# Cross-attention on Trainium2: probabilities transposed on TensorE, or in 32x32 blocks on VectorE and carried through DRAM

## What is computed

```python
q = _split_heads(hidden_states @ Wq.T, H)                  # (2, 20, 2048, 32)
k = _split_heads(text @ Wk.T, H); v = _split_heads(text @ Wv.T, H)
out_text = _merge_heads(_attend(q, k, v, sm_scale))        # softmax(q k^T / sqrt(32)) v
k_ip = _split_heads(ip @ Wk_ip.T, H); v_ip = _split_heads(ip @ Wv_ip.T, H)
out_ip = _merge_heads(_attend(q, k_ip, v_ip, sm_scale))
out = (out_text + IP_SCALE * out_ip) @ Wo.T + bo + residual
```

## Time and profile before

| | |
|---|---|
| median of 3 runs | 603.59 us |
| the profiled execution's own time | 606.17 us |
| its span in the trace | 604.1 us |
| PE busy | 583.6 us (97%) |
| DVE busy | 445.9 us (74%) |
| ACT busy | 312.6 us (52%) |
| POOL busy | 311.0 us (51%) |
| DMA, mean over the span | 76 GB/s |

### The profile page before, as it was taken

One profiled execution on the slowest core, in us unless ns is written; L12 is line 12 of the kernel. 1 busy time (PEld: TensorE's weight loads), 2 busy tenths in 40 slices (PEclk: granted clock), 3 DMA queues, 4 the chain that ended last, 5 costly groups with the idle time before them and its releaser, 6 DMA issues.

```text
span 604.1 us, 14571 instructions
## 1 busy us (share of the span) xinstructions
PE 583.6 (97%) x5634; PEld 516.3 (85%) x5634; DVE 445.9 (74%) x576; ACT 312.6 (52%) x594; POOL 311.0 (51%) x341
## 2 busy tenths in 40 slices
PE   8997878999999999999999999999999999999988
PEld 7997757888888888888888888888888888888867
DVE  0028576888788888878888887888888888788872
ACT  0223644565646555565655565555555565645541
POOL 0033436455574656475555647564746555574460
PEclk9998898999999999999999999999999999999999
DMA  8992001112121212112121212121211212111101
GB/s 296 414 374 79 1 1 28 63 36 88 44 81 44 87 35 82 39 46 76 43 87 35 86 39 84 35 87 43 68 53 35 87 35 87 44 37 44 36 18 62
DMA packets 29401, 46.20 MB, mean 76 GB/s; under 512 B 3392, under 2 KB 24512, under 8 KB 29120
## 3 DMA queue, kind: packets, MB, share of 16 engines
q1 hardware_dynamic: 29376, 45.84, 22.3%
HBM read 35.34 MB, written 10.49 MB: 76 GB/s over the span
## 4 chain that ended last, share of the span: by engine, by line
PE 92%; DVE 3%; ACT 2%; DMA 1%; issue 1%; SPq 0%; POOL 0%; ACTq 0%
PE q_ps L580 23%; PE x_ps L580 22%; PE main_ps L616 11%; PE s_ps L604 9%; PE pv_ps L635 8%; PE pv_ps L633 7%; PE s_ps L725 3%; PE pv_ps L624 3%; PE pv_ps L725 2%; PE main_ps L725 1%; DMA stage<-wk_in 1%; DVE row_sum L503 1%; ACT probs L363 1%; PE s_ps L672 1%; ACT p_main L368 1%
## 5 line engine op out<-in xcount | busy, mean ns | idle before, releaser
L305 POOL TENSOR_TENSOR probs<-probs,row_inv 128x616 f32<-128x616 f32 (+1 forms) x160 | 159.7, 1020 | 228.9 <-DVE row_inv L506 228.9
L503 DVE TENSOR_REDUCE row_sum<-probs 128x16 f32<-128x1232 f32 x80 | 114.9, 1436 | 45.7 <-ACT probs L363 45.7
L363 ACT ACTIVATE probs<-probs 128x616 f32<-128x616 f32 x160 | 113.8, 719 | 60.4 <-DVE probs L495 60.4
L368 ACT ACTIVATE p_main<-main_ps 122x512 f32<-122x512 f32 x160 | 94.3, 589 | 88.4 <-PE main_ps L616 88.1
L487 DVE TENSOR_REDUCE row_max<-s_ps 128x16 f32<-128x1232 f32 x80 | 115.3, 1441 | 31.7 <-PE s_ps L604 31.7
L495 DVE TENSOR_TENSOR probs<-s_ps,row_max 128x616 f32<-128x616 f32 x160 | 120.5, 795 | 2.7
L616 PE MATMUL main_ps<-ident,probs 128*122 128x128 f32 x640 | 96.1, 273 | 4.5 <-ACT p_main L368 4.5
L580 PE MATMUL q_ps<-x_hi,wq_hi 128*128 128x256 f32 x400 | 88.9, 320 | 0.0
L387 ACT ACTIVATE attn_hi<-pv_ps 128x256 fp32r<-128x256 f32 x80 | 30.9, 387 | 91.4 <-PE pv_ps L635 91.0
L616 PEld LDWEIGHTS main_ps<-ident,probs 128*122 128x122 f32 x640 | 73.1, 138 | 6.0 <-ACT p_main L368 5.9
L580 PE MATMUL x_ps<-attn_hi,wo_hi 128*128 128x256 f32 x375 | 75.5, 299 | 0.8 <-ACT y L382 0.8
(11 more groups left out here) (71 smaller groups left out, 774.0 us busy)
## 6 DMA issues: line engine op xcount, KB each, us to landing
x_raw<-x_in SPq DMA_DIRECT2D x16, 640.0 KB, 3.8
res<-x_in SPq DMA_DIRECT2D x75, 128.0 KB, 2.0
y_out<-res SPq DMA_DIRECT2D x75, 128.0 KB, 1.7
stage<-wk_in SPq DMA_DIRECT2D x6, 640.0 KB, 8.2
stage<-wv_in SPq DMA_DIRECT2D x6, 640.0 KB, 9.7
wq_raw<-wq_in SPq DMA_DIRECT2D x1, 1600.0 KB, 10.1
wo_raw<-wo_in SPq DMA_DIRECT2D x1, 1600.0 KB, 7.3
stage<-wk_in SPq DMA_DIRECT2D x4, 320.0 KB, 5.8
```

Of the source, the lines that this page charges most:

```text
L305: nc.gpsimd.tensor_tensor(rows[:, :, keys], rows[:, :, keys], row_inv[:, u.slot, :, br].unsqueeze(2) .broadcast_to([P, GROUP * SUB, size]) ...
L363: nc.scalar.activation(probs[:, u.slot, heads], probs[:, u.slot, heads], ACT.Exp).then_inc(exp_done, 1)
L368: nc.scalar.activation(p_main[0:MAIN, :, s * P:(s + 1) * P], main_ps[0:MAIN].rearrange("p (j n) -> p j n", j=GROUP), ACT.Copy).then_inc(ma ...
L503: nc.vector.tensor_reduce(row_sum[:], by_row(probs[:, u.slot].rearrange("p j s n -> p j (s n)")), AXIS.X, ALU.add).then_inc(sum_done, 1)
```

## The change

All 154 keys now take one other way. `normalise` writes all of the second branch. DVE then turns the probabilities of a unit in 32x32 blocks (`turn`, three instructions, into `turned`): each block of 32 query rows and 32 keys is transposed in place of its four partition groups. One DMA (`bounce`) writes the 640 KB of `turned` to the DRAM tensor `bounce_d`, and eight DMAs (`load_turned`) read it back: four of 128 KB into `p_main`, which put the 32 keys of each of four blocks on their own 32 partitions, and four of 32 KB into `p_rest`, for the last 26 keys of each head, padded to 32. All nine are issued by SP. The transposes of PE, their identity operand and `keep_main` of ACT, `keep_rest` of DVE and `normalise_rest` of POOL are gone. `weigh_values` reads `p_main` and `p_rest` with strides, and now works on unit `u-3`; the output chunk is that of `u-8`.

The softmax is split by heads: for the first two heads ACT reads `s_ps` itself, in eight instructions of 77 keys, with the negated row maximum as bias and the row sum as accumulator output (`exp_direct`). The other two heads go as before, through one `take_max` and one `exp`; DVE sums only these. `find_max` is two instructions of two heads each.

```diff
-REST = D
-MAIN = BLK - REST
+BLOCKS = P // D
+MAIN = BLOCKS * D
+REST = BLK - MAIN
+ROW = GROUP * SUB * D
 VALUES = 2 * BATCHES
 PASSES = 3
 STEPS_OF_PRODUCT = PASSES * GROUPS
-OUT_LAG = 6
+OUT_LAG = 8
+VALUE_LAG = 3
 Q_AHEAD = 2
 PAIR = 2
-HALF = D // 2
+PARTS = 3
...
+        probs_flat = sbuf("probs", [P, 2, GROUP * SUB * BLK + MAIN])
+        probs = probs_flat[:, :, 0:GROUP * SUB * BLK].rearrange("p i (j s n) -> p i j s n", j=GROUP, s=SUB)
+        turned = sbuf("turned", [P, 2, BLOCKS + 1, GROUP * SUB, D])
+        p_main = sbuf("p_main", [P, GROUPS, BLOCKS, GROUP, SUB, D])
+        p_rest = sbuf("p_rest", [P, GROUPS, BLOCKS, SUB, D])
+        bounce_d = nc.dram_tensor("bounce_d", (GROUPS, P, BLOCKS + 1, ROW), F32, kind="Internal").ap()
...
+            def bounce(u):
+                wait(sp, p_turned, u.number(PARTS, PARTS))
+                sp.dma_start(bounce_d[u.g].rearrange("p b n -> p (b n)"),
+                             turned[:, u.slot].rearrange("p b q k -> p (b q k)")).then_inc(bounced, DMA)
+            def load_turned(u):
+                wait(sp, bounced, u.number(DMA, DMA))
+                for b in range(BLOCKS):
+                    sp.dma_start(p_main[rows_of(b), u.g].rearrange("k a j s n -> k a (j s n)"),
+                                 bounce_d[u.g, :, b].rearrange("(a k) n -> k a n", a=BLOCKS)
+                                 ).then_inc(p_loaded[u.g], DMA)
+                for j in range(GROUP):
+                    cols = slice(j * SUB * D, (j + 1) * SUB * D)
+                    sp.dma_start(p_rest[rows_of(j), u.g].rearrange("k a s n -> k a (s n)"),
+                                 bounce_d[u.g, :, BLOCKS, cols].rearrange("(a k) n -> k a n", a=BLOCKS)
+                                 ).then_inc(p_loaded[u.g], DMA)
             def emit(u):
                 ahead, old, new = u.tile_plus(2), u.plus(-OUT_LAG - 2), u.plus(GROUPS - OUT_LAG - 3)
+                if u.plus(-2).exists():
+                    load_turned(u.plus(-2))
                 if new.exists() and not (new.fixed and new.number() >= LAST.number()):
                     load_residual(new)
                 if old.exists():
                     store(old)
+                if u.plus(-1).exists():
+                    bounce(u.plus(-1))
                 if u.g == 2 and ahead.exists():
                     wait(sp, x_lo_done, u.tile(1, 2))
                     sp.dma_start(x_raw[:], x_d[ahead.t, ahead.batch]).then_inc(x_loaded, DMA)
...
+            final = LAST.plus(GROUPS - 1)
+            load_residual(LAST.plus(-1))
+            store(LAST.plus(-5))
+            load_turned(final.plus(-1))
+            store(LAST.plus(-4))
+            bounce(final)
+            store(LAST.plus(-3))
+            load_turned(final)
+            store(LAST.plus(-2))
...
-                for br, keys in enumerate((slice(0, KEYS), slice(KEYS, MAIN))):
+                for br, keys in enumerate((slice(0, KEYS), slice(KEYS, BLK))):
...
-            def exp(u, half):
-                heads = slice(half * PAIR, (half + 1) * PAIR)
-                wait(act, s_drained, u.number(2, half + 1))
-                nc.scalar.activation(probs[:, u.slot, heads], probs[:, u.slot, heads], ACT.Exp).then_inc(exp_done, 1)
-            def keep_main(u, s):
-                wait(act, main_turned, u.number(SUB, s + 1))
-                nc.scalar.activation(p_main[0:MAIN, :, s * P:(s + 1) * P],
-                                     main_ps[0:MAIN].rearrange("p (j n) -> p j n", j=GROUP), ACT.Copy
-                                     ).then_inc(main_kept, 1)
+            def exp_direct(u):
+                wait(act, max_done, u.number(2, 1))
+                for j in range(PAIR):
+                    rows = probs[:, u.slot, j].rearrange("p s n -> p (s n)")
+                    for i in range(SUB * BRANCHES):
+                        cols = slice(i * KEYS, (i + 1) * KEYS)
+                        done = nc.scalar.activation(rows[:, cols], s_ps[:, j, cols], ACT.Exp,
+                                                    bias=row_neg[:, j, i:i + 1], accum_out=row_sum[:, j, i:i + 1])
+                done.then_inc(direct_done, 1)
+            def exp(u):
+                wait(act, sub_done, u.number(1, 1))
+                rows = probs[:, u.slot, heads_of(1)]
+                nc.scalar.activation(rows, rows, ACT.Exp).then_inc(exp_done, 1)
...
-                ahead, nxt, last = u.tile_plus(2), u.plus(Q_AHEAD), u.plus(-1)
+                ahead, nxt = u.tile_plus(2), u.plus(Q_AHEAD)
                 chunk = u.plus(-OUT_LAG)
-                if u.plus(-2).exists():
-                    attn_high(u.plus(-2))
-                exp(u, 0)
-                if chunk.exists():
-                    exp(u, 1)
-                    keep_main(last, 0)
-                else:
-                    keep_main(last, 0)
-                    exp(u, 1)
+                exp_direct(u)
+                exp(u)
+                if u.plus(-VALUE_LAG).exists():
+                    attn_high(u.plus(-VALUE_LAG))
                 if nxt.exists():
                     keep_q(nxt)
-                keep_main(last, 1)
                 if chunk.exists():
                     add_bias(chunk)
...
-            def find_max(u):
-                wait(dve, s_ready, u.number(1, 1))
-                nc.vector.tensor_reduce(row_max[:], by_row(s_ps[:, :, 0:SUB * BLK]), AXIS.X, ALU.max
-                                        ).then_inc(max_done, 1)
-            def take_max(u, half):
+            def find_max(u, half):
                 if half == 0:
-                    wait(dve, max_done, u.number(1, 1))
-                heads = slice(half * PAIR, (half + 1) * PAIR)
+                    wait(dve, s_ready, u.number(1, 1))
+                nc.vector.tensor_reduce(row_neg[:, heads_of(half)], by_row(s_ps[:, heads_of(half), 0:SUB * BLK]),
+                                        AXIS.X, ALU.max, negate=True).then_inc(max_done, 1)
+            def take_max(u):
+                wait(dve, max_done, u.number(2, 2))
+                heads = heads_of(1)
                 nc.vector.tensor_tensor(by_row(probs[:, u.slot, heads].rearrange("p j s n -> p j (s n)")),
                                         by_row(s_ps[:, heads, 0:SUB * BLK]),
-                                        row_max[:, heads].unsqueeze(3).broadcast_to([P, PAIR, SUB * BRANCHES, KEYS]),
-                                        ALU.subtract).then_inc(s_drained, 1)
+                                        row_neg[:, heads].unsqueeze(3).broadcast_to([P, PAIR, SUB * BRANCHES, KEYS]),
+                                        ALU.add).then_inc(sub_done, 1)
+            def turn(u, part):
+                wait(dve, p_done, u.number(BRANCHES, min(part + 1, BRANCHES)))
+                if part == 0:
+                    wait(dve, bounced, u.number(DMA, -DMA))
+                first, end = (0, 2, BLOCKS, BLOCKS + 1)[part:part + 2]
+                rows = probs_flat[:, u.slot, first * D:first * D + GROUP * SUB * BLK].rearrange("p (q n) -> p q n", n=BLK)
+                nc.vector.transpose(turned[:, u.slot, first:end],
+                                    rows[:, :, 0:(end - first) * D].rearrange("p q (b k) -> p b q k", k=D)
+                                    ).then_inc(p_turned, 1)
             def invert(u):
-                wait(dve, exp_done, u.number(2, 2))
-                nc.vector.tensor_reduce(row_sum[:], by_row(probs[:, u.slot].rearrange("p j s n -> p j (s n)")),
+                wait(dve, exp_done, u.number(1, 1))
+                nc.vector.tensor_reduce(row_sum[:, heads_of(1)],
+                                        by_row(probs[:, u.slot, heads_of(1)].rearrange("p j s n -> p j (s n)")),
                                         AXIS.X, ALU.add).then_inc(sum_done, 1)
                 wait(dve, sum_done, u.number(1, 1))
+                wait(dve, direct_done, u.number(1, 1))
                 nc.vector.reciprocal(row_inv[:, u.slot].rearrange("p (j s) r -> p j (s r)", j=GROUP), row_sum[:]).then_inc(inv_done, 1)
...
             def emit(u):
-                find_max(u)
                 for half in range(2):
-                    take_max(u, half)
-                if u.plus(-2).exists():
-                    attn_low(u.plus(-2))
+                    find_max(u, half)
+                take_max(u)
+                if u.plus(-1).exists():
+                    for part in range(PARTS):
+                        turn(u.plus(-1), part)
                 invert(u)
-                keep_rest(u.plus(-1))
+                if u.plus(-VALUE_LAG).exists():
+                    attn_low(u.plus(-VALUE_LAG))
...
                 wait(pe, q_done, u.number(1, 1))
-                wait(pe, s_drained, u.number(2))
+                wait(pe, direct_done, u.number())
...
+            def weigh_values(u):
+                wait(pe, p_loaded[u.g], u.tile((BLOCKS + GROUP) * DMA, (BLOCKS + GROUP) * DMA))
+                wait(pe, attn_lo_done, u.number())
```

(31 more changed lines are left out.)

135 lines of the change are left out of this document (59 added, 76 removed).

## The result

The changed kernel takes **739.33 us**, the median of four runs (736.46 to 741.58), against 603.24 (602.09 to 605.25) for the kernel before in the same comparison: a ratio of 1.2243 (in brackets here and below, the 95% interval: [1.2194, 1.2292]), slower by 136 us. Forecast were 730 us, with 650 to 875 as the range. The profiled execution took 738.83 us, with a span of 737.0.

A forecast was written before the change was run, and what follows sets the result against it. SP's queue was taken to bound the kernel: each bounce's landing plus issuing made 8.3 us a unit. First bounce at 64.2, rounds to 713.9, 8.6 to the last load and 5.9 of tail, plus 2.1, gave 730 us; range 650 to 875.

The forecast's parts named there:

- PE loses 1.10 us a unit: PE's list without the transposes: 1.10 us a unit removed, 6.59 falling to 5.49; 88 us less if PE still set the pace.
- DVE: the size: DVE's work per unit after the change: 6.07 us (5.6 to 6.9), with 1.79 for the three transposes, from 5.57 before.
- ACT: the time: ACT's eight exp instructions of 77 keys: 2.55 us a unit, ACT then having at most 5.74 a unit.
- The upper bound of 5.1: Upper price of ACT's eight instructions, 5.1 us, if the accumulator output doubles each one.
- SP's round: SP's list per unit: landing 3.5, wait 0.1, eight loads 3.68, residual and store 1.0; 8.3 us, setting the pace.
- the sum: Whole-kernel time: first bounce at 64.2, SP's rounds to the last bounce at 713.9, then the tail; span 728.4, forecast 730 us.
- So the lag would be enough: Loop through DRAM over three units: 18.5 / 3 = 6.2 us a unit, so the lag hides it; SP's order does not.
- Late landing: Rival: the bounce lands late under load, 1.8 us a unit more, 142 us more, 872; chance 0.14.
- Dear issue: Rival: SP's loads cost 0.61 us each to issue, round 9.7 us, time 841; chance 0.10.
- Cheap issue: Rival: SP issues the quarter loads cheaply, at 0.2 us each, round 6.2, time 585, faster than before; chance 0.05.
- Clock: Rival: PE's waits lower its granted clock; given no chance, only 0.2 us a unit, 16 us, inside the range.
- What would show it: Signs: SP's loads 0.46 us apart, a unit every 8.3 us, PE about 65% busy in mid-run, waiting at the values.

## Why the prediction was right, point by point

**PE loses 1.10 us a unit: right.** Its list is 5.50 us (the run with 16 dummy matmuls), forecast 5.49. In the changed kernel none of it reaches the end.

**DVE: the size was 0.7 too high.** Busy 428.8 / 80 = 5.36 us a unit against 6.07. The transposes took 686, 686 and 403 ns, 1.78 us together against 1.79, so the price of the elements was right. The copy of `p_rest`, 0.42, was named as going and never subtracted. Nothing hung on it.

**ACT: the time right, the reason half right.** The eight take 302.39 to 304.81, 2.42 us, against 2.55. The accumulator output is an instruction of its own of 216 ns; it overlaps its neighbours, so a pair starts every 0.30 us. The upper bound of 5.1 was far off. The price had neither the read nor the overlap in it, and that these two nearly cancel is luck. The Trainium skill ("ScalarE: Activation LUTs", section "What ACT_TABLE_LOAD costs") lets neighbours overlap by some 93 ns, which gave an estimated 2.1; here the trace does not agree, for between two neighbours the accumulator read stands.

**SP's round: right in its make-up, and in its sum partly by luck.** Eight issues took 3.64 against 3.68, with starts 0.46 apart. Landing and wait took 3.23 against 3.6, 0.37 too much in the forecast; residual and store took 1.11 and the 0.26 ahead of them against 1.0, 0.37 too little. The two cancel: 8.24 against 8.3. That the terms add up, which the forecast rested on, is what the experiments show: more issues cost 0.46 each, half the bytes of the loads nothing, and the landing taken out of the list gave 84 us and more. They add up nearly, not exactly: with four issues fewer the landing grew, and 124 us came back instead of 146.

**What the sum missed: 9 us.** The first bounce went at 63.73 (forecast 64.2), the ninth at 125.85 (124.6), the last at 719.75 (713.9): the rounds with `x_raw`, for which the sum had no term, are most of it, and the run with the small `x_raw` gave 6 us back; the other rounds were a little shorter than forecast, 8.23 in the mean. The last bounce to the last values took 8.46 (8.6). Behind them the end took 737.0 - 728.21 = 8.8 instead of 5.9. Most of this last is the clock: the timeline of PE, the values of the last unit but one and of the last,

```profile
720.77 0.64 PE L658 MATMUL pv_ps<-p_main,v 128*32 128x256 f32 x8 [0.51 <-DMA p_rest<-bounce_d]
...
728.21 0.97 PE L658 MATMUL pv_ps<-p_main,v 128*32 128x256 f32 x8 [2.58 <-DMA p_rest<-bounce_d]
```

shows the same eight matmuls at 0.64 and, after a wait of 2.58 us, at 0.97, with the 15 output matmuls behind them 0.21 us apart instead of 0.12, 1.4 us for these alone. The granted clock from 728 us to the end is 0.52, nearly all at the lower of its two levels. No later wait of PE is left there that could take it up.

**"So the lag would be enough": this step failed.** The loop over three units was put at 18.5 / 3 = 6.2 us. With the landing out of SP's list it set the pace at 7.2, and a fourth unit of lag gave 65 us. Read from the starts of 65 units of that run, the loop is 21.7 us in the mean, against 18.5: from the bounce to its first load 4.3 (forecast 3.6; SP had its own residual and store to issue, and the bounce landed after 3.6 in the median), from the first load to the values 7.3 (forecast 3.2 + 1.7 = 4.9), from the values to the scores 5.3 (5.5), from the scores to the bounce 4.8 (4.5). So the step that was too short is that from the loads to the values: `p_rest` landed after 3.0 us instead of 1.7 (its page, median), and issues were slower (one `p_rest` quartet took 2.60 us). The forecast of 730 did not hang on it, since 8.3 was larger either way; the expectations of the runs with the bounce on ACT did.

**The rivals.** *Late landing* did not come: 3.2 us at 203 GB/s. It needed more load: 4.0 us in the median at 263 GB/s with the engines 90% busy, and some 8 us beside an `x_raw`. The Trainium skill ("DMA: Bandwidth & Descriptors", section "Latency and other measured facts") has HBM answer in 2 us at high load; no run here shows DRAM's own answer, only the whole transfer, whose median grew by 0.8 us. *Dear issue* did not come in this version (0.46), but it did where the bounce is queued just ahead of the loads (0.6 a load). *Cheap issue* did not come. *Clock* cost nothing in mid-run, as forecast, and some 2 to 3 us at the end.

**What would show it.** Loads 0.46 apart, a unit in 8.36, PE's waits at the values: as said, but these are 165.1 / 77 = 2.1 us, not 2.8. PE was busy 75% in mid-run, not about 65%. At least part of that is the lower clock, at which the same work fills more of the wait: a matmul of the first query product, just behind the values, took 377 ns in the mean against 320 before, one of the last output product 283 as before.

## What to carry to other kernels

A queue that waits for its own transfer makes that transfer's latency a step of its list: before judging a detour through DRAM, look what stands between an issue and the wait for its landing, and move the wait one unit later or the issue to another queue (118 and 84 us here, 149 together). Count issues of the queue, 0.46 us each here from 32 to 128 KB while little is queued, before bytes. And split by size: here the large part of the probabilities through DRAM in four loads and the small rest on PE, at 0.31 us a unit, made 554 us out of 604 and 739.

## What the runs showed of the hardware that was not expected

- Issuing slows down with what is queued. Four loads of 128 KB took 1.75 us to issue when the bounce ahead of them had landed, and 2.46 right behind a bounce of 640 KB.
- An activation with an accumulator output is followed by a read of 216 ns, which overlaps the activations around it: a pair starts every 0.30 us, though the two last 335 and 216.
- The granted clock fell to 0.91 in mid-run although PE was busy 269 of 360 us, and to 0.79 in the last 37 us; it rose to 0.98 with 1.4 us more work a unit. It falls for short stretches: after PE's wait of 2.21 us that ended at 303.70 it was 0.78 from 304 to 306 and 0.50, the lower level, from 306 to 308.
- Five times as many DMAs a unit as before (11.2 against 2.2) brought the DMA engines to a busy share of 0.90 at 263 GB/s, where 425 GB/s had been moved at 1.01: the share at a given rate is higher with these transfers. The page of the run with the bounce on ACT and the lag of 4 tells the bounces from the rest, for they alone are on ACT's queue, `q10` (packets, MB, share of 16 engines' span of 590.6 us):

```profile
q1 hardware_dynamic: 121536, 98.31, 60.7%
q10 hardware_dynamic: 11520, 52.43, 23.5%
```

The writes to DRAM moved 52.43 MB in 0.235 x 590.6 us, at 378 GB/s while busy; the rest, mostly the loads, 98.31 MB in 0.607 x 590.6, at 274. So a byte of the loads took more of the engines' time than a byte of the writes to DRAM. Without the `p_rest` loads, whose rows are 256 bytes, the same queue comes to 312 (87.81 MB in 52.1% of 540.4). Rows of 512 instead of 1024 bytes cost nothing in the changed kernel: 63.9% of 737.0 us for SP's queue, and 52.9% of 884.0 with eight loads of `p_main`, both some 470 us.
